# Loads issued a stage ahead, and the experts' inputs split ahead of half of their second weights

## What is computed

```
x = x + tanh(g_xattn[0]) * attention_0(layernorm(x), ctx)
x = x + tanh(g_ffn[0])   * experts_0(layernorm(x))      # 8 experts, top 2, gelu, biases
x = x + tanh(g_xattn[1]) * attention_1(layernorm(x), ctx)
x = x + tanh(g_ffn[1])   * experts_1(layernorm(x))      # 7 experts and a no-op, top 2, capacity 256, relu
```

## Time and profile before

| | |
|---|---|
| median of 3 runs | 851.69 us (850.74 to 852.61) |
| the profiled execution | 850.55 us, of which the span of the trace is 848.8 us |
| PE busy | 753.4 us, 89% of the span |
| PEld busy | 636.0 us, 75% |
| DVE busy | 604.8 us, 71% |
| ACT busy | 477.6 us, 56% |
| POOL busy | 395.0 us, 47% |
| mean granted clock of TensorE | 0.952 of full speed |
| HBM | 84.22 MB read, 17.83 MB written |

### The profile page before, as it was taken

One profiled execution on the slowest core, in us unless ns is written; L12 is line 12 of the kernel. 1 busy time (PEld: TensorE's weight loads), 2 busy tenths in 40 slices (PEclk: granted clock), 3 DMA queues, 4 the chain that ended last, 5 costly groups with the idle time before them and its releaser, 6 DMA issues. The chain is left out here.

```text
span 848.8 us, 17412 instructions
## 1 busy us (share of the span) xinstructions
PE 753.4 (89%) x6872; PEld 636.0 (75%) x6872; DVE 604.8 (71%) x1212; ACT 477.6 (56%) x722; POOL 395.0 (47%) x379
## 2 busy tenths in 40 slices
PE   6999999999369999999999966999999999459995
PEld 6666667677369999999999966666667677359995
DVE  4777777743769888988988933777776743749882
ACT  3376666763156776766766632486666753435640
POOL 6365443112145757666667335365443112063642
PEclk9999999999679999999999997999999999669998
DMA  7001000001367877887877527001000001489632
GB/s 230 20 16 39 27 27 27 25 30 51 109 244 243 243 219 249 254 251 218 261 222 224 161 25 230 15 14 40 27 27 27 27 27 50 152 233 282 195 87 27
DMA packets 47697, 103.45 MB, mean 122 GB/s; under 512 B 9952, under 2 KB 38240, under 8 KB 39936
## 3 DMA queue, kind: packets, MB, share of 16 engines
q0 software_dynamic: 18912, 67.56, 27.8%
q1 hardware_dynamic: 28704, 34.78, 12.2%
HBM read 84.22 MB, written 17.83 MB: 120 GB/s over the span
## 5 line engine op out<-in xcount | busy, mean ns | idle before, releaser
L598 DVE TENSOR_REDUCE mx_a<-ps_max_a 128x2 f32<-128x512 f32 x256 | 164.2, 685 | 35.4 <-PE ps_max_a L844 35.2
L89 PE MATMUL ps_h_e<-xe_t_e,w_e 128*128 128x256 f32 (+1 forms) x480 | 138.2, 288 | 16.2 <-DVE xe_t_e L1750 16.2
L450 ACT ACTIVATE prob_a<-ps_st_a 128x2048 f32<-128x2048 f32 x64 | 120.1, 1877 | 29.0 <-PE ps_st_a L863 28.5
L90 PE MATMUL ps_h_e<-xe_t_e,w_e 128*128 128x256 f32 (+1 forms) x480 | 135.1, 281 | 0.0
L91 PE MATMUL ps_h_e<-xe_t_e,w_e 128*128 128x256 f32 (+1 forms) x480 | 135.1, 281 | 0.0
L89 PE MATMUL ps_y_e<-w_e,h_e 128*128 128x256 f32 x424 | 118.2, 279 | 0.0
L90 PE MATMUL ps_y_e<-w_e,h_e 128*128 128x256 f32 x424 | 117.7, 278 | 0.0
L91 PE MATMUL ps_y_e<-w_e,h_e 128*128 128x256 f32 x424 | 117.7, 278 | 0.0
L89 PEld LDWEIGHTS ps_h_e<-xe_t_e,w_e 128*128 128x128 f32 x480 | 93.2, 194 | 18.6 <-DVE xe_t_e L1750 18.6
L90 PEld LDWEIGHTS ps_h_e<-xe_t_e,w_e 128*128 128x128 f32 x480 | 92.9, 194 | 0.0
L91 PEld LDWEIGHTS ps_h_e<-xe_t_e,w_e 128*128 128x128 f32 x480 | 92.8, 193 | 0.0
(11 more groups left out here) (236 smaller groups left out, 1758.6 us busy)
## 6 DMA issues: line engine op xcount, KB each, us to landing
w_raw_w<-L_w SPq DMA_DIRECT2D x14, 1024.0 KB, 7.2
ctx_raw_a<-ctx_t SPq DMA_DIRECT2D x16, 256.0 KB, 3.7
normalised_weighted<-xr SPq DMA_DIRECT2D x16, 256.0 KB, 2.2
x_sb<-x SPq DMA_DIRECT2D x8, 256.0 KB, 4.4
x_sb<-x SPq DMA_DIRECT2D x2, 1024.0 KB, 8.3
x<-x_sb SPq DMA_DIRECT2D x8, 256.0 KB, 2.5
out<-x_sb SPq DMA_DIRECT2D x8, 256.0 KB, 2.5
out<-xr POOLq DMA_DIRECT2D x4, 512.0 KB, 11.1
```

The costliest lines, as they stand in the source:

```text
L89: pe.matmul(out, lhs[0], rhs[0], start=start, stop=False)
L90: pe.matmul(out, lhs[1], rhs[0], start=False, stop=False)
L450: act.activation(prob[n % 2][:, :, :, :], ps_st[:, :, :, :], ACT.Exp, scale=HD ** -0.5).then_inc(prob_ready, 1)
L598: dve.tensor_reduce(mx[:, q, h:h + HG + 1:HG], ps_max[j][:, :, :], AX.X, ALU.max).then_inc(max_done, 1)
```

## The change

- The raw attention weights no longer have tiles of their own; they lie in the upper half of `xr`. Their semaphores, and one for x, are made for the whole program and cleared once at its end.
- Layer 0: x of batch 0, wq and wk are loaded in the constants stage, behind the gates. wv and wo are loaded where they were.
- Layer 1: all four attention weights are loaded in the expert stage of layer 0, when four blocks have their y.
- VectorE's `route_constants` moves from ahead of `moments(0)` to behind `moments(2)`; `fill_first(24)` becomes 12 in layer 0.
- Experts, both layers: at jp 3 the inputs of the next block are split ahead of the second half of w2, on ScalarE and on VectorE.
- Experts, layer 0: the gelu table load and the inputs of block 0 stand ahead of w1 of block 1.
- Experts, layer 1: SP waits for the gathered rows of blocks 0 and 1 before it loads the weights that follow the first three.

```diff
@@ attention_phase
-        w_raw = {n: sb(f"{n}_raw", [P, KC, D]) for n in ("wq", "wk", "wv", "wo")}
+        w_raw, first_ld = shared["w_raw"], shared["first_ld"][layer]
...
-            load_x(0)
-            load_weight("wq", wq_ld)
+            if layer:
+                load_x(0)
             sp.dma_start(bq[:, :], dram["bq"]).then_inc(wq_ld, 16)
             load_context(0)
-            load_weight("wk", wk_ld)
             sp.dma_start(bk[:, :], dram["bk"]).then_inc(wk_ld, 16)
             load_x(1)
-            load_weight("wv", wv_ld)
+            if layer == 0:
+                load_weights_early(sp, 0, shared, dram, ("wv",))
             sp.dma_start(bv[:, :], dram["bv"]).then_inc(wv_ld, 16)
             load_context(1)
             load_x(2)
             sp.dma_start(bo[:, :], dram["bo"]).then_inc(wo_ld, 16)
-            load_weight("wo", wo_ld)
+            if layer == 0:
+                load_weights_early(sp, 0, shared, dram, ("wo",))
...
             def weight_high(n):
-                act.wait_ge(loads[n], 32)
+                act.wait_ge(first_ld[n], 16)
...
             def moments(b):
-                if b < XP:
+                if b == 0 and layer == 0:
+                    dve.wait_ge(first_ld["x"], 16)
+                elif b < XP:
                     dve.wait_ge(x_ld[b], 16)
...
-            if layer == 0:
-                route_constants()
             moments(0)
             normalise_rows(0)
...
             moments(1)
             moments(2)
+            if layer == 0:
+                route_constants()
             values(0)
...
-            fill_first(24)
+            fill_first(24 if layer else 12)
@@ new, and constants_phase
+def load_weights_early(sp, layer, shared, dram, names):
+    for n in names:
+        sp.dma_start(shared["w_raw"][n][:, :, :],
+                     dram[f"L{layer}_{n}"].rearrange("(k p) n -> p k n", p=P)).then_inc(shared["first_ld"][layer][n], 16)
...
             sp.dma_start(gates[:, :], dram["gates"]).then_inc(g_ld, 16)
+
+            src = dram["x"].rearrange("(t p) d -> p t d", p=P)
+            sp.dma_start(shared["x"][:, 0:QT, :], src[:, 0:QT, :]).then_inc(shared["first_ld"][0]["x"], 16)
+            load_weights_early(sp, 0, shared, dram, ("wq", "wk"))
@@ expert_phase, sync_part
         if layer:
+
+            for b in range(2):
+                sp.wait_ge(xe_ld[b], passed(b))
+
             def load_weights(b):
...
+        if layer == 0:
+
+            sp.wait_ge(y_ready, 4)
+            load_weights_early(sp, 1, shared, dram, ("wq", "wk", "wv", "wo"))
@@ expert_phase, act_part
         for b in range(2):
             for k in range(KC):
                 w1_high(b, k)
-        if layer == 0:
-            act.activation(unread[:, :], shared["tanh_g"][:, 0:1], ACT.Gelu)
-        inputs_high(0)
+            if b == 0:
+                if layer == 0:
+                    act.activation(unread[:, :], shared["tanh_g"][:, 0:1], ACT.Gelu)
+                    inputs_high(0)
+        if layer:
+            inputs_high(0)
         for b in range(blocks):
             for jp in range(NP):
+                if jp == (NP - 1 if b else 1) and b + 1 < blocks:
+                    inputs_high(b + 1)
                 if jp < KC:
                     if b and b + 1 < blocks:
                         w1_high(b + 1, jp)
                 else:
                     w2_high(b, jp - KC)
-                if jp == (NP - 1 if b else 1) and b + 1 < blocks:
-                    inputs_high(b + 1)
@@ expert_phase, dve_part
         for b in range(2):
             for k in range(KC):
                 w1_low(b, k)
-        inputs_low(0)
+            if b == layer:
+                inputs_low(0)
         for b in range(blocks):
             for jp in range(NP):
+                if jp == (NP - 1 if b else 1) and b + 1 < blocks:
+                    inputs_low(b + 1)
...
-                if jp == (NP - 1 if b else 1) and b + 1 < blocks:
-                    inputs_low(b + 1)
                 hidden_parts(b, jp)
@@ program
+        sem = semaphores(nc, ctx)
...
+        shared["w_raw"] = {n: shared["xr"][:, TT // 2 + KC * i:TT // 2 + KC * (i + 1), :] for i, n in enumerate(("wq", "wk", "wv", "wo"))}
+        shared["first_ld"] = [{n: sem(f"{n}_first{layer}") for n in ("x", "wq", "wk", "wv", "wo")} for layer in range(2)]
```

More of the change, by code:

```diff
@@ L213, in _ @@
             ctx_src = dram["ctx_t"].rearrange("(k p) n -> p k n", p=P)
-            w3 = {n: dram[n].rearrange("(k p) n -> p k n", p=P) for n in ("wq", "wk", "wv", "wo")}
             def load_context(b):
@@ L232, in load_x @@
                 sp.dma_start(x[:, tiles, :], src[:, tiles, :]).then_inc(x_ld[i], 16)
-            def load_weight(n, done):
-                sp.dma_start(w_raw[n][:, :, :], w3[n]).then_inc(done, 16)
-            load_x(0)
-            load_weight("wq", wq_ld)
+            if layer:
+                load_x(0)
             sp.dma_start(bq[:, :], dram["bq"]).then_inc(wq_ld, 16)
             load_context(0)
-            load_weight("wk", wk_ld)
             sp.dma_start(bk[:, :], dram["bk"]).then_inc(wk_ld, 16)
             load_x(1)
-            load_weight("wv", wv_ld)
+            if layer == 0:
+                load_weights_early(sp, 0, shared, dram, ("wv",))
             sp.dma_start(bv[:, :], dram["bv"]).then_inc(wv_ld, 16)
@@ L409, in queries @@
                 if b == 0:
-                    act.wait_ge(wq_ld, 32)
+                    act.wait_ge(wq_ld, 16)
                 project(b, q_ps, q_evac, bq, q_s[b % 3][0])
@@ L414, in keys @@
                 if b == 0:
-                    act.wait_ge(wk_ld, 32)
+                    act.wait_ge(wk_ld, 16)
                 project(b, k_ps, k_evac, bk, k_c[b % 2])
@@ L456, in heads @@
                 act.activation(head_t[n % 2][:, :, :], ps_head[:, :].rearrange("p (c s) -> p c s", c=2), ACT.Copy).then_inc(head_out, 1)
-            loads = {"wq": wq_ld, "wk": wk_ld, "wv": wv_ld, "wo": wo_ld}
             def weight_high(n):
-                act.wait_ge(loads[n], 32)
+                act.wait_ge(first_ld[n], 16)
                 act.activation(w[n][0][:, :, :], w_raw[n][:, :, :], ACT.Copy).then_inc(w_hi[n], 1)
             def scale_bias():
-                act.wait_ge(wo_ld, 32)
+                act.wait_ge(wo_ld, 16)
                 act.activation(tgbo[:, :], bo[:, :], ACT.Copy, scale=tg).then_inc(tgbo_ready, 1)
@@ L584, in values @@
                     dve.wait_ge(value_ones_set, 1)
-                    dve.wait_ge(wv_ld, 32)
+                    dve.wait_ge(wv_ld, 16)
                 dve.wait_ge(v_ps, b + 1)
```

## The result

The changed kernel takes 849.0 us (median, 846.94 to 853.07) where the kernel before takes 850.87 (848.57 to 853.98): ratio 0.9977, 95% interval 0.9966 to 0.9987. It is faster by 1.9 us, about what can be told from no change. The forecast was a gain of 15.5 us, 836.2, in a range of 831.0 to 842.0: it was wrong. The profiled execution took 847.42 us with a span of 845.7, 3.1 us less than before.

The account below looks back on a forecast made before the run. TensorE was taken to idle for stage-specific reasons: xe_t inputs, gathered rows, first x rows. Terms 8.0 + 1.2 + 1.5 + 1.2 + 3.0 + 0.3 + 0.7 - 0.4 = 15.5 us off 850.55 gave 835.05, median 836.2, range 831.0 to 842.0.

Parts of the forecast that it names:

- 1: Layer 0's experts: inputs ahead of half of w2 shrink six small-block gaps, 8.0 us, and the third block's gap, 1.2.
- 2: Layer 0's experts: TensorE's clock no longer falls after the longest gap, gain 1.5 us, bounds 0 and 1.5.
- 3: Layer 0's first expert block: inputs and table load ahead of the second w1, gain 1.2 us, bounds 0.5 and 1.7.
- rival C: VectorE stays the experts' bound (1 gives half, -4.0) or early start runs at slow clock (-2.3): 838.5 to 842.5; 15%.
- rival D: POOL becomes the pacemaker, its w2 gather waiting on a later b2 copy: 866.4 us by the median; 3%, 2% in part.
- 4: Kernel start: x, wq and wk loaded earlier, route constants behind the moments; first queries 3.0 us earlier, bounds 0.7 and 3.3.
- 5: Start of layer 1: four weight loads gone from the start, gain 0.3 us, bounds 0 and 0.6.
- 6: Layer 1's experts: earlier first rows and reorder gain 4.3 us at best, later adds lose 3.0; middle taken, 0.7.
- rival B: Layer 1's experts: weights delay the adds, block 3's rows land up to 3.0 us later, 6 is -3.0: 839.9; 15%.
- 7: End of kernel: one more barrier to clear the stage-spanning semaphores, loss of 0.4 us, bounds 0 and 0.9.

Follow-up runs that it names:

- Run 3: Kernel before with only the reorder: next block's inputs split ahead of half of w2, on ScalarE and VectorE; 840.5 us, ratio 0.9891.
- run 11: 7 with layer 0's route constants moved near the attention stage's end and GpSimd's context 1 split behind the second batch's normalised rows; 831.18 us.
- 2: Changed kernel with GpSimd held at the start of layer 1's attention until VectorE has normalised the first rows; 846.13 us, ratio 0.995.
- 8: Changed kernel with GpSimd's four adding transfers issued ahead of the first row gathers, SP's wait kept, GpSimd not held; 837.57 us, ratio 0.984.
- 9: Kernel before with layer 1's load of context 0 issued ahead of that of wq; 853.7 us, ratio 1.0036.
- 1: Changed kernel without SP's wait for the gathered rows ahead of layer 1's weight loads; 839.96 us, ratio 0.9881.
- 4: Kernel before with only SP's wait for the rows of blocks 0 and 1 added; 858.82 us, ratio 1.0104.
- 7: 2 with the four adding transfers of xr issued ahead of the first row gathers, SP's wait kept; 831.92 us, ratio 0.9806.

## Why the prediction was wrong, point by point

**1, 2, 3: right.** The six gaps after small blocks are 0.29 to 0.45 us (0.2 to 0.5 was said), the clock behind each is 1.00, and the first block gained 1.13 of 1.2. Run 3 shows the reorder worth 9 to 10 us alone. VectorE had the room, so the first half of rival C did not come, and neither did rival D, though GpSimd's waits for the b2 copy went from 43.1 to 55.4 us.

**4: right up to the first queries, then 0.85 short.** The first moments started at 4.66 and the queries at 10.88, 3.04 us earlier. The step that failed was the cover of the route constants ("behind the moments they fall in the idle time of 4.99 us ahead of the values"): they were hidden on VectorE, but not from GpSimd beside it, whose copy of the queries took 1.61 us in place of 0.62. GpSimd's normalised rows came only 1.55 us earlier than before, and TensorE waited 0.78 for them, until 19.84. I had followed the chain to the first queries and no further. At the transposes of a later batch's rows (52.60 us before, 50.38 after) the lead of 3.04 us is 2.22, less by about that wait. In run 11, where the wait is gone, they start at 49.24, and the lead of 3.36 us at the queries is whole.

**5: wrong by 3.2.** I priced what the loads that were gone had cost, and found nearly nothing. I didn't ask what the load behind them, context 0, would set going: GpSimd's work came 0.5 us earlier and, with no pause in it, took VectorE's place at the head of the chain. The 0.73 us of VectorE's pair were a duration taken from rows in which the pair started 0.4 to 0.5 us ahead of GpSimd. Runs 2, 8 and 9 show it from both sides. The Trainium skill states in "GPSIMD Engine Reference", section "Specifications", that GpSimd's SBUF interfaces are shared with VectorE, with contention for VectorE's instructions in a two-port mode or with two SBUF inputs; "SBUF — State Buffer", section "SBUF: two separate sides", adds that the one that starts first holds the port for its instruction and the other blocks. This case's trace agrees that the two delay each other, and is harsher than one instruction's length: VectorE's pair of 0.73 us ended 2.7 us late, behind three of GpSimd's in a row. That a port is the reason no run shows.

**6: wrong, the sum's +0.7 against some -7.1 (the stage's -7.51 less the barrier's 0.4).** The half of it on the first rows was right: they landed in 3.58 us where 7.30 stood, and the first product came 3.3 us sooner after the next stage's fill. The half on the adds was right in kind: rival B's mechanism is what happened, and runs 1 and 4 show it by its removal and by its addition. Its price was the failed step: "3 MB more beside them, 7.2 us at 416 GB/s, less what runs before 752, give an end about 3.0 us later". Counted from the stage's first fill, the adds ended at 53.9 us before and at 61.4 after, 7.5 us later. Two things in that step were wrong.

The first is the share. The step shares the DMA by bytes, but the queues share it by packets: 125 of GpSimd's, of 1.0 KB, for 120 of SP's, of 8.2 KB, so GpSimd's queue got an eighth of the bytes. The trace of before had a sign of it. From 768 to 772 us, some three of them beside weights, its queues read

```profile
q1 hardware_dynamic: 130, 1.01, 61.9%
q0 software_dynamic: 301, 0.35, 47.8%
```

against 0.77 MB alone. The second is the number of loads. In the kernel before, the adds, issued from 755.72 on, had the engines to themselves until SyncE's next load at 764.14; three loads of 1 MB met their last part, and they were done at 776.8, after 21.1 us. In the changed kernel, issued from 741.79 on, they met seven (three issued at 739.3 to 740.2, then one each at 750.41, 754.81, 759.88 and 765.06, as buffers came free) and were done by 773.7, when the rows behind them landed, after 31.9 us. The prediction counted only the first three. Rows of before would have priced the four loads more: in four microseconds with one such load the adds move 0.35 MB in place of 0.77, so four loads leave 1.7 MB to do, 9 us at 0.19 MB per us; 10.8 were measured. The rule of the Trainium skill that the prediction weighed ("DMA: Bandwidth & Descriptors", "Queues, rings and completion order") agrees with these packet counts: taking turns a packet at a time, as it states, gives about equal counts, and 125 and 120 were measured. I turned it into a number with the wrong rows. On top came TensorE's clock, 0.54 of full for the 4.18 us after the gap.

**7: right.** SyncE waited ten times at barriers, 5.0 us in all, where it had waited nine times, 4.6 us: 0.4.

The chances failed with the bounds. A case of -7 had no place among the rivals (the worst for item 6 was -3.0, at 15%), so "faster by over 0.2%" was given 0.95 for a kernel that is faster by 0.2%.

## What to carry to other kernels

Before a wait is added that lets one transfer go first, list what the held-back transfers will meet later, and take the shares from a stretch where those two queues ran together; a queue of small packets can crawl at less than a quarter of its pace beside one of large ones (0.04 MB per us against 0.19 here), and what else stands in that queue crawls with it. When a load comes earlier, ask which engine it wakes and beside whose instruction, since GpSimd and VectorE delay each other. Work moved out of one engine's way must be looked for where it lands, at the far end of the stage too. A change of several edits that moves little should be split at once: here one edit alone was worth more than all together.

## What the runs showed of the hardware that was not expected

- GpSimd's four adding transfers of 512 KB took 8.7 us each to land (median) when sent ahead of the rows and the held-back weights (7), 11.0 with the rows before them (1), and 21.8 beside the held-back weights (after).
- A queue's share beside another went by packets, one for one: 0.13 MB of 1.0 KB packets for 0.98 MB of 8.2 KB packets in 3 us.
- Of two instructions on VectorE and GpSimd that overlap, either can be the one delayed. VectorE's cast of 128x2048 integers made one of GpSimd's instructions about 1.0 us longer, a different one in each execution: the copy (1.61 in place of 0.61 us) in most, the tiny 128x2 scale in 1 (1.18 in place of 0.22). GpSimd's unbroken run made VectorE's pair 3.41 or 3.42 us long in all four profiles in which context 0 was early and nothing held GpSimd (after, 1, 8, 9).
- A wait of TensorE of 0.8 us near 20 us was followed by a clock of 1.00, waits of 1.3 by 1.00 in two profiles, but one of 1.2 by 0.83, one of 1.5 by 0.83 and one of 1.76 by 0.66. So the length of the wait alone doesn't settle whether the clock falls. In the three profiles with the fall, attention of layer 0 ended 1.5, 1.8 and 2.5 us later than in the changed kernel's.
